# Pool's wait for a whole group of gathered edges: kept in layer 1, taken out of layer 0

## The reference

```python
xn = layernorm(x)                                            # 3125 x 256
agg_h = segment_sum((xn * norm_out[:, None])[src], dst)      # gather 50000 rows, add by dst
agg_e = segment_sum(edge_attr_64, dst)
gnn = relu((concat([agg_h, agg_e], 1) @ weight) * norm_in[:, None] + bias)
h = logmap0(proj(xn));  h = relu(batchnorm(conv1d(h, w_qkv)))        # 3125 x 768
t = logmap0(proj(expmap0(h)));  s = grouped_convs(t)                 # 3125 x 768 each
mix = hyperbolic_linear_attention(concat([t, s])) @ w_res + b_res
x = x + gnn + mix
x = x + moe_0(layernorm(x))                                  # 8 experts, top 2
# layer 1: the same plan, with edge weights in the segment sum
```

## Time and profile before

| | us |
|---|---|
| runs, median of 3 | 2357.14 (2355.99 to 2359.45) |
| the profiled execution | 2355.14 |
| its span | 2353.1 |
| stage qkv_channels, from Pool's first instruction in it to PE's first of the mixer | 78.42 to 253.03 |
| stage mixer, from PE's first instruction in it to the last product of a group | 253.03 to 633.48 |
| PE busy over the span | 1849.0 (79%) |
| DVE busy over the span | 1246.6 (53%) |
| Pool busy over the span | 911.5 (39%) |

### The profile page before, as it was taken

How to read it: one execution, slowest core, us unless ns; L and a number is a source line. 1 busy time by engine, 2 the same in 40 slices (tenths; PEclk the granted TensorE clock), 3 DMA queues, 4 the chain that set the end, 5 groups by cost and what they waited for, 6 DMA issues and landing times. The chain is left out here.

```text
span 2353.1 us, 35048 instructions
## 1 busy us (share of the span) xinstructions
PE 1849.0 (79%) x10583; PEld 1437.1 (61%) x10584; DVE 1246.6 (53%) x3264; ACT 710.1 (30%) x1624; POOL 911.5 (39%) x933
## 2 busy tenths in 40 slices
PE   6589668666465899999975998768888684799976
PEld 5355446444253799999962565535656472688875
DVE  6644676766456444444458556633443376333345
ACT  5222333333342122112127931122222132133324
POOL 0555555555320222222220435555655300254542
PEclk9999889888777799999996999969999897799997
DMA  7544444444264011011113323333333317211224
GB/s 228 143 120 123 127 113 113 117 109 111 77 271 164 27 32 33 31 34 35 35 46 126 104 92 103 95 102 95 103 102 103 95 55 303 107 62 64 64 58 148
DMA packets 171236, 239.46 MB, mean 102 GB/s; under 512 B 74145, under 2 KB 139261, under 8 KB 168692
## 3 DMA queue, kind: packets, MB, share of 16 engines
q0 software_dynamic: 42336, 112.74, 16.7%
q1 hardware_dynamic: 116884, 113.45, 14.8%
q10 hardware_dynamic: 11904, 11.96, 1.6%
HBM read 184.86 MB, written 56.12 MB: 102 GB/s over the span
## 5 line engine op out<-in xcount | busy, mean ns | idle before, releaser
L655 POOL DMA_INDIRECT agg_message<-table,edges_src x638 | 626.8, 982 | 617.3 <-DMA agg_message<-table,edges_src 264.2
L2822 PEld LDWEIGHTS ex_p_h<-ex_xT,ex_own_up 128*128 128x128 f32 (+1 forms) x2464 | 281.3, 192 | 2.7 <-issue 1.4
L2822 PE MATMUL ex_p_h<-ex_xT,ex_own_up 128*128 128x128 f32 (+1 forms) x2464 | 282.0, 276 | 1.0 <-DVE ex_xT L2873 1.0
L714 PE MATMUL agg_partial<-agg_message,moe_up 128*64 128x321 f32 x638 | 124.6, 533 | 117.0 <-issue 95.8
L2877 DVE COPY ex_own_up<-moe_up 128x1280 f32 x114 | 100.5, 883 | 168.7 <-PE ex_p_h L2822 167.9
L2781 POOL DMA_INDIRECT ex_x<-moe_in,route_token_at x58 | 57.4, 989 | 311.9 <-PE ex_p_x L2812 242.3
L714 PEld LDWEIGHTS agg_partial<-agg_message,moe_up 128*64 128x64 f32 x638 | 53.0, 161 | 163.3 <-issue 144.0
L714 PE MATMUL agg_partial<-agg_message,agg_onehot 128*64 128x256 f32 x638 | 97.2, 446 | 66.0 <-issue 55.3
L726 ACT COPY agg_span<-agg_partial 128x321 f32<-128x321 f32 (+1 forms) x108 | 43.2, 400 | 336.4 <-PE agg_partial L718 286.7
L2865 ACT ACTIVATE ex_gate_h<-ex_p_h 128x640 f32<-128x640 f32 x56 | 39.5, 705 | 315.3 <-PE ex_p_h L2822 315.3
L3018 ACT COPY ex_own_up<-moe_up 128x1024 f32 x66 | 67.5, 1044 | 213.4 <-PE ex_p_h L2991 163.2
(11 more groups left out here) (665 smaller groups left out, 3684.0 us busy)
## 6 DMA issues: line engine op xcount, KB each, us to landing
moe_up<-in_f_w SPq DMA_DIRECT2D x8, 1386.0 KB
agg_message<-in_edge_rows SPq DMA_DIRECT2D x54, 192.0 KB
agg_message<-table,edges_src POOLq DMA_INDIRECT x638
sums<-agg_span SPq DMA_DIRECT2D x107, 80.2 KB
moe_up<-in_f_w SPq DMA_DIRECT2D x4, 2048.0 KB, 15.3
moe_down<-in_f_w SPq DMA_DIRECT2D x4, 2048.0 KB
sums<-agg_span SPq DMA_DIRECT2D x107, 64.0 KB
moe0b_down<-in_f_w SPq DMA_DIRECT2D x8, 768.0 KB
```

The lines of the kernel that those rows point to most:

```text
L655: pool.indirect_dma_start(out=to[:, k * w:k * w + D], out_offset=None, in_=self.table, in_offset=bass.IndirectOffsetOnAxis(ap=self.edges.s ...
L714: mm = pe.matmul(self.partial[h * W:(h + 1) * W, 0:w], hot[:, k * W:(k + 1) * W], msg[:, k * w:(k + 1) * w], start=(k % RUN == 0), stop=(g ...
L2822: return pe.matmul(to, own_up[:, o:o + n], xT[:, k * D + c * P:k * D + (c + 1) * P], start=(c == 0), stop=(c == 1))
```

## The change

The wait for the landing of group g-1 is issued only where the object was built with `apart=True`, and only layer 1's is. Layer 0 is built without it. Nothing else differs; the helper `landed` is gone, so that later lines have numbers lower by three.

```diff
-    def __init__(self, nc, ctx, tag, edges, table, sums, cleared, width, weighted, edge_rows=None, onehot=None, ring=RING):
+    def __init__(self, nc, ctx, tag, edges, table, sums, cleared, width, weighted, edge_rows=None, onehot=None, ring=RING, apart=False):
         m = Memory(nc, ctx, tag)
-        self.ring = ring
+        self.ring, self.apart = ring, apart
...
-    def landed(self, pool, g, n):
-        pool.wait_ge(self.gathered[g % self.ring], (g // self.ring * GE + n) * 16)
-
     def gather(self, pool, g):
         if g >= self.ring:
             pool.wait_ge(self.used, g - self.ring + 1)
         to, w = self.slot(self.message, g, self.width), self.width
-        if g:
-            self.landed(pool, g - 1, len(self.tiles(g - 1)))
+        if g and self.apart:
+            pool.wait_ge(self.gathered[(g - 1) % self.ring], ((g - 1) // self.ring * GE + len(self.tiles(g - 1))) * 16)
...
-                edge_sums = EdgeSums(nc, inner, "agg1", edges, table1, sums1, cleared[1], D, True, ring=RING + 1)
+                edge_sums = EdgeSums(nc, inner, "agg1", edges, table1, sums1, cleared[1], D, True, ring=RING + 1, apart=True)
```

## The result

The changed kernel takes 2336.9 us (median of four runs, 2333.8 to 2340.0) against 2358.0; the ratio is 0.9917, with a 95% interval of 0.9904 to 0.993. It is faster by about 20 us. I had forecast 80, with a range that ended at 2304. The profiled execution took 2337.1, 18.0 less than the one before; its span is 2335.0.

A forecast was written before the change was run, and what follows sets the result against it. Pool's pace, with its waits for landings, was taken to bound the mixer. Gains of 4 + 18 + 61.5 - 4 = 79.5 off 2355.1 gave 2275.6, as median 2277; likeliest 2267 to 2287, range 2264 to 2304.

The forecast's parts named there:

- The barrier before the mixer: End of qkv_channels: Pool's last group there begins earlier, so the barrier moves by 3.3 to 5.8 us, taken as 4.
- The mixer up to make_head: From the mixer's start to make_head: without late groups make_head starts near 338, not at 356.06, a gain of 18 us.
- from make_head on: Group 26's products to group 52's: 188.9 us at Pool's pace in place of 250.4, a gain of 61.5.
- 24 groups, 29 to 52, at 7.58: After make_head: Pool issues these groups without landing waits at 7.58 us each, 181.9 us together.
- Costs looked for: Whom denser gathers hit in the mixer: DMA engines 55% busy, stores little, DVE's port under 4 us, already counted.
- tile 5: Mixer before make_head: its product came 17.84 us after tile 4's, 7.06 of them a wait for squares that would go.
- Are the other engines that fast?: Group 26 to 52: PE's chain without its waits would take 172 us, so Pool stays the bound by some 17.
- DVE holds Pool: Rival, chance 0.13: DVE's products hold Pool's gathers, costing 14 us after make_head and 3 at the barrier; gain 62, 2295.
- The stores fall behind: Rival, chance 0.04: gathers without a pause slow SP's stores in the mixer, 12.7 us a group, about 2400.
- The stock never forms: Rival, chance 0.09: Pool's lead is gone at each two-group tile, 219 us after make_head in place of 189; 2307.
- No change: Rival, chance 0.02: DVE's work covers all of PE's waits in the mixer, only the barrier's 4 us won: 2353.
- My own sign for being wrong: In the mixer: Pool waiting for slots all through the second half would mean that DVE or PE sets the pace.

The follow-up runs named there:

- 5.2 alone: The kernel before, with the landing wait dropped only for groups 1 to 16, gathered in qkv_channels, and kept in the mixer: 2352.9 us, ratio 0.9985.
- pause_per_gather: The changed kernel plus a 0.39 us memset of an unused tile by Pool after every gather of layer 0: 2306.2 us, ratio 0.9792.
- half_gathers: The changed kernel, but from the fourth group of layer 0 on three gathers a group in place of six: 2240.0 us, ratio 0.9502.
- few_features: The changed kernel, but from the fourth group on edge features of one tile of six are loaded: 2339.3 us, ratio 0.9936.
- pause_per_group: The changed kernel plus an iota into an unused tile by Pool ahead of each group of layer 0: 2356.8 us, ratio 1.0011.

## Why the prediction was wrong

**What bounded the kernel.** Right in the main: Pool's rhythm set the mixer's pace. Not seen: the kernel before already had some of the slow steps (35.0 us of such waits at ACT, in six gathers in a row). It fits this that spreading the gathers gained more than any way of handling the wait.

**The barrier before the mixer** was put at 4, within 3.3 to 5.8; it measured 5.5, and 5.2 alone. That it stayed under 5.8 was luck: this bound took DVE's long product to stay where it was, and it did so only because DVE had waited for ACT, and ACT for PE's signal, as their timelines in the changed kernel show. The last two lines are DVE's product and PE's first products in pause_per_gather:

```profile
237.57 0.69 ACT L1034 COPY moe_up<-qkv_p_out 128x640 f32<-128x640 f32 x1 [6.64 <-remote]
...
238.30 0.89 DVE L972 BATCH_NORM_STATS2 layer_stats<-moe_up 128x6 f32<-128x320 f32 x2 [8.53 <-ACT moe_up L1034]
...
242.62 3.48 DVE L991 TENSOR_TENSOR layer_XN<-layer_XN,mapping_share 128x3200 f32<-128x3200 f32 x1
...
229.96 3.48 DVE L997 TENSOR_TENSOR layer_XN<-layer_XN,mapping_share 128x3200 f32<-128x3200 f32 x1
...
238.82 3.48 PE L717 MATMUL agg_partial<-agg_message,moe_up 128*64 128x321 f32 x12 [8.57 <-PEq L111]
```

There the product starts 12.7 us earlier than in the changed kernel, and the mixer's first products start at 238.8, 14 us earlier than before.

**The mixer up to make_head** was to gain 18 and lost 9.6, and **from make_head on** brought 19.8 of 61.5. Both fail at the same step, and it is not the one that I doubted. "24 groups, 29 to 52, at 7.58" takes a group's gathers, once free of the wait, to cost no other engine anything. Under *Costs looked for* I asked whom the denser gathers hit and named the DMA engines, the stores and DVE's port. They hit the instructions of PE and SP, and PE's signals, for which ACT and Pool wait. So Pool could not run at 7.58 per group: the slots came free late, 82 us of waits, and from group 26's products to group 52's it took 230.6 us where the sum had 188.9. DVE's waits show it for the part ahead of make_head (two lines before, 254 to 356; one after, 248 to 360). The wait of 7.1 that the forecast took off tile 5, for ACT's squares, is gone as it should be. In its place DVE waited 30.6 us for the work that ACT does once make_cat's signal is there, near the 27.6 between the 18 won and the 9.6 lost.

```profile
DVE mix_prod L1176 <- ACT mix_square L1258: 7.1, 1, 7.1
DVE mix_size L1156 <- ACT mix_kr L1236: 2.5, 1, 2.5
...
DVE mix_size L1153 <- ACT mix_kr L1233: 30.6, 3, 18.2
```

**Are the other engines that fast?** Yes, by half_gathers: 175.9 us against 172, and 83.5 us from the mixer's first products to make_head, where the forecast had 338 - 249 = 89 (249 is 253.03 less the 4 of the barrier).

**The rivals.** *DVE holds Pool* explains little: the mixer's 217 gathers took 210.72 us in place of 207.96, the longest 1.424 in place of 1.337.

The Trainium skill's rule (SBUF — State Buffer, section "SBUF: two separate sides") would have taken 14 us at full price; 2.8 is what the gathers show of it at the most. The prediction read this section too widely: what it says of descriptors goes for DVE's two-port modes, and for an operation with two inputs in SBUF, as the marks and the long product are, it names only a GpSimd operation that reads SBUF. Which of the two held the 4.28 us gather no run here shows.

*The stores fall behind* did not happen: SP waited 2.7 us for the stores before, against 8.4. *The stock never forms* did not happen: after make_head PE waited 10.8 us for groups, and it was Pool that waited for slots. How the stock would do at 7.58 us per group without slow steps no run shows; half_gathers halves Pool's work. *No change* was wrong, but nearest to the time. My own sign for being wrong, Pool waiting for slots all through the second half, came true; the explanation that I gave for it, DVE or PE as the pace, did not.

**What stays open** is by which way Pool's gathers slow the others. The runs leave the gather that Pool issues, whatever it fetches, as the cause, and a limit over 1.42 us and near 1.50 for each. Whether PE's matmuls themselves end late or only their signals, the trace tells in part. Its semaphore events have the signals of make_cat, of the products and of make_res at 451.43, 451.57 and 451.66. The products and make_res take 1.84 + 0.82 + 1.89 = 4.55 us in the earlier trace rows, and cannot have been run in the 0.24 us between these signals; so make_cat's signal, at least, came over 4 us after its work. DVE's signals were not held: that of its operation from 444.91 to 445.60 came at 445.62. For the rest of make_cat's 12 us the question is open.

The Trainium skill says why PE's rows can't settle it (Perfetto Trace Analysis, section "Per-instruction lifecycle: what the profiler-reported window actually captures"): the end of a matmul in the profile is computed from its size and not observed. The rows agree: make_cat is over by 439.4 in the record, and its signal is seen at 451.4.

Every run on record has a span and a granted clock from the profiler, so whether the recording takes part in the slow steps was not tried. The number of transfers recorded does not bring them by itself: from 380 to 560 us few_features moved 11322 packets and had slow steps, pause_per_gather 24841 and had none.

## What to carry to other kernels

A wait that looks like lost time may be what spaces an engine's transfers: before it is taken out, ask what the denser issue does to engines that share no data with it, and try a small pause in its place. Here 0.38 us of idle work after each gather, in place of the wait, was worth 46 us in one layer and 89 in both, while taking the wait out of one layer was worth 20, and out of both left the kernel 37 slower than before. Gaps inside a run of matmuls that wait for nothing, and a signal that comes long after the work that gives it, are the signs.

## What was not expected of the hardware

- Indirect gathers issued by Pool each 1.25 us for longer than one group bring PE and SP down to one instruction per 0.7 us and hold back PE's signals up to 12 us, until Pool's queue has no packets left (451.1 in the stretch shown). At 1.42 us per gather about half of ACT's waits is left, at 1.50 less than a sixth, at 1.58 nothing.
- It does not depend on the bytes (a quarter of them: 99.7 us of waits against 94.3), nor on the rows (half of them: 99.1).
- A gather of 64 rows holds Pool nearly as long as one of 128: a median of 0.900 us against 0.946.
- An iota of 128x768 took 2.53 us in the kernel before, ahead of qkv_channels, and 0.77 in the loop of pause_per_group.
